# A four-layer graph network: the first layer's sums with all 14 cells' rows of a pair of batches gathered by TensorE, without indirect DMAs

## What is computed

```
def spmm(edge_row, edge_col, edge_val, m):
    gathered = edge_val[:, None] * m[edge_col]
    return jax.ops.segment_sum(gathered, edge_row, num_segments=N_NODES)
h = jax.nn.relu(spmm(edge_row, edge_col, edge_val, x @ W1))
out = spmm(edge_row, edge_col, edge_val, h @ W2)
x = _layernorm(x + out)
...
x = _layernorm(x + _L0_gnn_ref(x, src, dst, edge_weight, W1, W2))
x = _layernorm(x + _L1_gnn_ref(...))   # typed edges
x = _layernorm(x + _L2_gnn_ref(...))   # weighted edges, tanh map
x = _layernorm(x + _L3_gnn_ref(...))   # attention
```

## Time and profile before

| | us |
|---|---|
| timed runs, median of 3 | 9364.93 |
| timed runs, lowest and highest | 9363.02, 9368.05 |
| profiled execution, span | 12999.9 |
| profiled execution, anything beside its span | not shown |
| busy in the profiled span: TensorE, VectorE, ScalarE, GpSimd | 9231.9, 6869.4, 3183.5, 5674.7 |

### The profile page before, as it was taken

One profiled execution on the slowest core, in us unless ns is written; L12 is line 12 of the kernel. 1 busy time (PEld: TensorE's weight loads), 2 busy tenths in 40 slices (PEclk: granted clock), 3 DMA queues, 4 the chain that ended last, 5 costly groups with the idle time before them and its releaser, 6 DMA issues. The chain is left out here.

```text
span 12999.9 us, 294862 instructions
## 1 busy us (share of the span) xinstructions
PE 9231.9 (71%) x88712; PEld 7531.3 (58%) x88762; DVE 6869.4 (53%) x25269; ACT 3183.5 (24%) x9441; POOL 5674.7 (44%) x5790
## 2 busy tenths in 40 slices
PE   5977777777777777677777774888873555555555
PEld 5866667776766667634454453666662444444443
DVE  8964444444444444456666665555544555555555
ACT  5841111112111111241111123111113233222223
POOL 3534444442444444305555551444442555555552
PEclk8888888888888888789999996888886555555555
DMA  1013333333333333462222223333332111111113
GB/s 50 28 47 90 91 89 89 88 90 105 90 89 90 89 88 90 95 217 69 67 67 66 67 70 110 101 104 102 101 94 70 39 39 39 39 39 39 39 39 61
DMA packets 962709, 999.47 MB, mean 77 GB/s; under 512 B 141701, under 2 KB 861933, under 8 KB 962093
## 3 DMA queue, kind: packets, MB, share of 16 engines
q1 hardware_dynamic: 774502, 616.47, 17.1%
q0 software_dynamic: 174720, 364.70, 12.9%
q10 hardware_dynamic: 13255, 16.19, 0.4%
HBM read 858.52 MB, written 144.69 MB: 77 GB/s over the span
## 5 line engine op out<-in xcount | busy, mean ns | idle before, releaser
L497 POOL DMA_INDIRECT ring<-att_table,idx x1592 | 1556.3, 978 | 1307.7 <-ACT idx L484 715.5
L1225 PE MATMUL psum<-ring 128*128 128x128 bf16 x21276 | 1547.8, 226 | 784.6 <-issue 766.3
L1225 PEld LDWEIGHTS psum<-ring 128*128 128x128 bf16 x21276 | 1281.3, 101 | 984.9 <-issue 927.9
L1162 DVE TENSOR_SCALAR ring<-sel,iota_col 128x640 bf16<-128x640 bf16 (+1 forms) x1576 | 487.0, 369 | 2368.2 <-remote 1627.6
L1240 PE MATMUL psum<-state 64*128 64x128 f32 x14112 | 1479.8, 356 | 208.9 <-issue 206.7
L1240 PEld LDWEIGHTS psum<-state 64*128 64x128 f32 x14112 | 1318.1, 261 | 345.7 <-issue 330.0
L1148 POOL DMA_INDIRECT ring<-gcn_table,idx x980 | 932.3, 951 | 1300.6 <-ACT idx L1197 996.0
L1679 POOL DMA_INDIRECT state<-rel_table,state x1120 | 1071.1, 956 | 981.8 <-ACT state L1779 657.6
L1148 POOL DMA_INDIRECT ring<-rows,idx x980 | 933.7, 953 | 1289.0 <-ACT idx L1197 993.2
L1169 DVE TENSOR_SCALAR state<-iota_row,state 128x128 f32<-128x128 f32 x5488 | 1457.2, 356 | 0.0
L1394 POOL DMA_INDIRECT state<-hyp_table,state x784 | 755.8, 964 | 855.3 <-ACT state L1471 650.6
(11 more groups left out here) (447 smaller groups left out, 15814.7 us busy)
## 6 DMA issues: line engine op xcount, KB each, us to landing
ring<-xparts SPq DMA_DIRECT2D x1332, 192.0 KB
ring<-srow SPq DMA_DIRECT2D x544, 128.0 KB
sel<-drow SPq DMA_DIRECT2D x394, 160.0 KB
sel<-drow SPq DMA_DIRECT2D x394, 128.0 KB
rel_table<-tout SPq DMA_DIRECT2D x98, 512.0 KB, 2.6
ring<-att_table,idx POOLq DMA_INDIRECT x1592
ring<-rows SPq DMA_DIRECT2D x56, 448.0 KB
xparts<-state SPq DMA_DIRECT2D x28, 672.0 KB, 3.6
```

Source lines behind the costliest of these rows:

```text
L497: pool.indirect_dma_start(out=ring[:, u, k, 0:width], out_offset=None, in_=table, in_offset=bass.IndirectOffsetOnAxis(ap=idx[:, u, k:k + 1 ...
L1162: ins = nc.vector.tensor_scalar(reach[u % 2][:, t, :], wanted[u], at[:, :], None, ALU.is_equal)
L1225: last = nc.tensor.matmul(rowsP[v][:, j * P:(j + 1) * P], reach[v][:, t, j * P:(j + 1) * P], xwin[u][:, t, i, :], start=(t + i == 0), stop ...
```

## The change

For every cell the gather now takes place on TensorE. `PC`, `JP` and `JQ` are gone; `wanted`, `reach`, `rowsP` and `got` have all 7 x 128 = 896 columns (`BC`) for both batches of a pair; GpSimd's block, ScalarE's `stage`, the buffers `fetched` and `fetch` and their filling go; `scatter` takes all rows from `got` and waits for no indirect DMA. The rest of `cell_pass` is the same. The diff, without a few lines of its context:

```diff
--- before.py
+++ after.py
@@ -45,16 +45,11 @@
 GC = 28
 GW = GC // 2
 HS = P // 2
-JQ = (2, 3)
-JP = (SJ - JQ[0], SJ - JQ[1])
-QA = (0, JQ[0])
-QP = JQ[0] + JQ[1]
 GB = -(-(-(-E // P)) // GC)
 assert GB % 4 == 0 and (GB + 1) * GC <= EC and AW * SW <= NPAD and AW <= P
 CELLS = SG * GB * SJ
 CT = -(-(CELLS + 2 * SJ) // P)
 BC = SJ * P
-PC = (JP[0] * P, JP[1] * P)
 TOP = TILES * P - SW
 OFF = 1.0e6
 FG = 7
@@ -634,8 +629,6 @@
         assert at + 8 <= RING * K * ROW5
         tout_flat = tout[:, :, :].rearrange("p a w -> p (a w)")
         iota256 = tout_flat[:, 2 * RELS * D - SW:2 * RELS * D]
-        FETCH = (SG * GB // 2 + 1) * QP
-        fetch = state[:, NPAD - FETCH:NPAD]
         spread = tout_flat[0:GC, 0:GC * P // 2].bitcast(BF16).rearrange("p (c e) -> p c e", e=P)
 
         PT = 2
@@ -982,17 +975,6 @@
                             to.rearrange("p (g j i) -> p g j i", j=SJ, i=FB),
                             cells(tabW)[:, :, FR + q * FB:FR + (q + 1) * FB, :].rearrange("p g i j -> p g j i"))
                     ins.then_inc(sem("made"), 1)
-                    dve.wait_ge(sem("tbuilt"), -(-(CT + FT) // 4))
-                    indirect = cells(node[:, 0:CELLS])[:, :, :, min(JP):SJ]
-                    c(nc.vector.tensor_tensor(
-                        indirect, indirect,
-                        gbase.unsqueeze(1).unsqueeze(3).to_broadcast([P, SG, GB, SJ - min(JP)]), ALU.add))
-                    pairs = node[:, 0:CELLS].rearrange("p (q v j) -> p q v j", v=2, j=SJ)
-                    lists = fetch[:, 0:SG * GB // 2 * QP].rearrange("p (q i) -> p q i", i=QP)
-                    for v in range(2):
-                        c(nc.vector.tensor_scalar(lists[:, :, QA[v]:QA[v] + JQ[v]], pairs[:, :, v, JP[v]:SJ],
-                                                  float(N - 1), None, ALU.min))
-                    c(nc.vector.memset(fetch[:, SG * GB // 2 * QP:FETCH], 0.0))
 
                 @block.tensor
                 def _(pe):
@@ -1086,9 +1068,8 @@
 
         after[0] = 2 * CELLS
         picks = [in_state(SJ * P).rearrange("p (j d) -> p j d", d=P) for _ in range(4)]
-        got = [in_state(PC[u % 2]) for u in range(4)]
-        assert after[0] <= NPAD - FETCH
-        wanted = [sel_flat[:, u * (BC // 2):u * (BC // 2) + PC[u % 2] // 2].bitcast(BF16) for u in range(4)]
+        got = [in_state(BC) for u in range(4)]
+        wanted = [sel_flat[:, u * (BC // 2):(u + 1) * (BC // 2)].bitcast(BF16) for u in range(4)]
 
         def in_ring(words):
             at, ring_at[0] = ring_at[0], ring_at[0] + words
@@ -1097,9 +1078,8 @@
 
         ring_at = [0]
         xwin = [in_ring(3 * D).bitcast(BF16).rearrange("p (t i f) -> p t i f", t=2, i=3) for _ in range(4)]
-        reach = [in_ring(PC[v]).bitcast(BF16).rearrange("p (t e) -> p t e", t=2) for v in range(2)]
+        reach = [in_ring(BC).bitcast(BF16).rearrange("p (t e) -> p t e", t=2) for v in range(2)]
         zeros_b = in_ring(256).bitcast(BF16)
-        fetched = [in_ring(JQ[u % 2] * D).rearrange("p (q f) -> p q f", f=D) for u in range(4)]
         SUMS = SJ * SW
 
         def cell_pass(table):
@@ -1109,7 +1089,7 @@
 
 
             sums = [psum[:, 2 * h:2 * h + 2, :].rearrange("p b c -> p (b c)")[:, 0:BC] for h in range(2)]
-            rowsP = [psum[:, 4 + 2 * v:6 + 2 * v, :].rearrange("p b c -> p (b c)")[:, 0:PC[v]]
+            rowsP = [psum[:, 4 + 2 * v:6 + 2 * v, :].rearrange("p b c -> p (b c)")[:, 0:BC]
                      for v in range(2)]
             LAST = SG * GB
             IT = GB // 4
@@ -1124,7 +1104,7 @@
                                      xparts[bass.ds(at, SW), :].rearrange("(t p) c -> p t c", p=P)
                                      ).then_inc(sem(f"xin{u}"), 16)
                         sp.wait_ge(sem("reach"), n + 1)
-                        sp.dma_start(wanted[u], drow[bass.ds(n * BC, PC[u % 2])].partition_broadcast(P)
+                        sp.dma_start(wanted[u], drow[bass.ds(n * BC, BC)].partition_broadcast(P)
                                      ).then_inc(sem(f"din{u}"), 16)
 
                     with sp.Fori(0, SG) as sg:
@@ -1136,22 +1116,6 @@
                             load(LAST + u, GB + u, u)
                         sp.wait_ge(sem(f"xin{u}"), (LAST // 4 + (u < 2)) * 16)
                         sp.wait_ge(sem(f"din{u}"), (LAST // 4 + (u < 2)) * 16)
-
-                @block.gpsimd
-                def _(pool):
-                    with pool.Fori(0, SG) as sg:
-                        with pool.Fori(0, IT) as it:
-                            for u in range(4):
-                                pool.wait_ge(sem("staged"), sg * GB + it * 4 + (u + 1))
-                                pool.sem_inc(sem("issued"), 1)
-                                for q in range(JQ[u % 2]):
-                                    pool.indirect_dma_start(
-                                        out=fetched[u][:, q, :], out_offset=None, in_=table,
-                                        in_offset=bass.IndirectOffsetOnAxis(ap=idx[:, u, q:q + 1], axis=0)
-                                    ).then_inc(sem(f"g{u}"), 16)
-                    for u in range(4):
-                        pool.wait_ge(sem(f"g{u}"), LAST // 4 * 16 * JQ[u % 2])
-                    pool.dma_reset(range(sem("g0").num, sem("g3").num + 1))
 
                 @block.vector
                 def _(dve):
@@ -1192,13 +1156,6 @@
 
                 @block.scalar
                 def _(act):
-                    def stage(n, u, at):
-                        act.wait_ge(sem("scat"), n + 1)
-                        nc.scalar.activation(idx[:, u, 0:JQ[u % 2]], fetch[:, bass.ds(at, JQ[u % 2])],
-                                             ACT.Copy).then_inc(sem("staged"), 1)
-
-                    for u in range(2):
-                        stage(u, u, QA[u])
                     with act.Fori(0, SG) as sg:
                         with act.Fori(0, IT) as it:
                             for u in range(0, 4, 2):
@@ -1208,9 +1165,6 @@
                                     act.wait_ge(sem("scat"), n + (v + 1))
                                     nc.scalar.activation(got[u + v], rowsP[v], ACT.Copy
                                                          ).then_inc(sem("got"), 1)
-                                for v in range(2):
-                                    stage(n + (v + 2), (u + v + 2) % 4,
-                                          sg * (GB // 2 * QP) + it * (2 * QP) + ((u // 2 + 1) * QP + QA[v]))
 
                 @block.tensor
                 def _(pe):
@@ -1219,7 +1173,7 @@
                         pe.wait_ge(sem("reach"), n + 5)
                         pe.wait_ge(sem(f"xin{u}"), loaded)
                         pe.wait_ge(sem("got"), n + 1)
-                        for j in range(JP[v]):
+                        for j in range(SJ):
                             for t in range(2):
                                 for i in range(3):
                                     last = nc.tensor.matmul(rowsP[v][:, j * P:(j + 1) * P],
@@ -1228,14 +1182,11 @@
                                                             start=(t + i == 0), stop=(t + i == 3))
                         last.then_inc(sem("gat"), 1)
 
-                    def scatter(n, u, fetches):
+                    def scatter(n, u):
                         pe.wait_ge(sem("got"), n + 3)
                         pe.wait_ge(sem("picked"), n + 1)
-                        own = JP[u % 2]
                         for j in range(SJ):
-                            if j == own:
-                                pe.wait_ge(sem(f"g{u}"), fetches)
-                            rows = got[u][:, j * P:(j + 1) * P] if j < own else fetched[u][:, j - own, :]
+                            rows = got[u][:, j * P:(j + 1) * P]
                             for h in range(2):
                                 last = nc.tensor.matmul(sums[h][:, j * P:(j + 1) * P],
                                                         rows[h * HS:(h + 1) * HS, :],
@@ -1262,8 +1213,7 @@
                                 pe.wait_ge(sem("sent"), sg + 1)
                                 clear(True)
                             for v in range(2):
-                                q = 16 * JQ[v]
-                                scatter(n + v, u + v, sg * (IT * q) + it * q + (at // 4 * q + q))
+                                scatter(n + v, u + v)
 
                     pe.sem_inc(sem("gat"), 4)
                     pe.sem_inc(sem("scat"), 4)
```

## The result

The changed kernel takes 10060.94 us (median of 4 runs, 10058.7 to 10064.46), against 9366.49 us for the kernel before (4 runs, 9363.02 to 9375.23): 694 us more, a ratio of 1.074 with a 95% interval of 1.0726 to 1.0755. The forecast was 10040, its range 9700 to 10150.

A forecast was written before the change was run, and what follows sets the result against it. TensorE was taken to bound the changed stage at 6.51 us a pair. Gathers +680, run-ahead gathers at the calls' starts +3.5 and setup -2.5 gave +681 on 9365, 10046, stated as 10040 us; range 9700 to 10150.

The forecast's parts named there:

- The bound: Changed stage, timed run: TensorE sets the pair's period at 6.51 us, GpSimd just behind at 6.25 us.
- that cover: Per pair of the changed stage: TensorE outlasts GpSimd's indirect DMAs by 0.26 us, so removing them gains nothing.
- rival A: GpSimd already bounds the timed pair, at 6.9 to 7.5 us; changed kernel 9655 to 9890 us; chance 0.13.
- T: True period of one pair in the changed stage before the change: taken as 6.51 us, at most 9.28.
- the 11.37 us of the table by stage: Recorded time a pair in the stretched profile: 4456 us over 392 pairs of the changed stage's two calls.
- rival B: TensorE's gaps during the gather are real, made by indirect DMAs; break-even or faster, 8957 at the limit; chance 0.10.
- (1): Gather on TensorE: 30 more matmuls a pair at 57.8 ns, 1.73 us unhidden, +680 us over 392 pairs.
- (6): GpSimd and ScalarE: 1960 indirect DMAs, 2450 us of GpSimd's time, and index copies go; costed at nothing.
- (3, 4): VectorE comparisons grow to 456 ns each, ScalarE copies to 927 ns, both hidden under the scatter.
- (5): Row loads: hardware queue grows from 2.65 to 3.3 us a pair, the software queue's 1.8 us goes.
- (7): Setup: four VectorE operations, 1.37 us, and three smaller go, about -2.5 us.

The follow-up runs named there:

- the first experiment: Kernel before, unedited, profiled a second time: the execution took 9365.33 us with a span of 9363.5 us.
- the changed kernel with spare fetches: Changed kernel plus five indirect DMAs a pair into a spare buffer nobody reads or waits for: 10056.54 us, ratio 1.074 to the kernel before.

## Why the prediction was right, point by point

- **The bound.** TensorE at 6.51 us, GpSimd at 6.25 behind it. Measured 6.446, the same without any indirect DMA; a sixth puts GpSimd in front. GpSimd's 6.25 was its quickest pace: under load its DMAs start 1.27 to 1.29 us apart, so it stood 0.1 us behind at most and not 0.26. The forecast did not hang on the size of that cover, but it was much nearer to rival A than the prediction thought. Taking T from the one pair without gaps was the step that carried everything; the 11.37 us of the table by stage would have led to rival B. That the other stages run in 0.80 of their recorded time was nearly right too: they were put at 6813 us and measure about 6755 (9363.5 less 1297.0 + 1298.5 and, behind each call's last gather, one pair). The two calls are some 56 us longer than the 2552 us put on them, by their starts and the 12 seams, which the prediction did not count; both kernels have these.
- **The gathers (1).** 30 x 57.8 ns = 1.73 us a pair. Measured 8.120 - 6.446 = 1.674 us, 55.8 ns a matmul, and the steps of six matmuls between four, five and six indirect DMAs give 55.7 and 55.8: a straight line with 3.43 us of the pair left for everything else. The prediction's 57.8 ns had taken a fixed part of the gather's 3.12 us into the price of a matmul. The difference is 22 us in the sum of 680. The Trainium skill's 81 ns ("TensorE: Matmul & The Clock Gate", "Back-to-back issue gap") would have given 953 us, and these rows disagree with it for this stream.
- **The removal (6), at nothing.** Shown from both sides: taken from the kernel before, 1.0004; put back into the changed one, no difference.
- **Comparisons and copies (3, 4).** 450 ns against 456, 918 against 927, and under the scatter as said. That TensorE would wait for comparisons at the starts and seams, the prediction did not see: 54.6 us in the changed kernel. The kernel before, in the trace without gaps, has 54.5, so the change adds nothing to it.
- **Queues (5).** 3.0 us a pair for 3.3 forecast.
- **The sum came out closer than its parts.** Between the traces of the first experiment and of the changed kernel lie 10056.5 - 9363.5 = 693.0 us. The two calls between their first and last gathers account for 661.0 us (1627.1 and 1629.4 against 1297.0 and 1298.5); what lies before the first of them for 3.0, where 2.5 less were forecast (7); what lies between the calls for 0.5; and 28.5 lie behind the second call's last gather, in stages that the change does not touch. One row shows the largest part, the indirect DMAs of the typed layer, in the kernel before and in the changed one (line, count, min/median/max ns, first and last start):

```profile
L1679 POOL DMA_INDIRECT state<-rel_table,state x1120: 938/944/1762, 3958.0 to 5485.8; - x187
```

```profile
L1629 POOL DMA_INDIRECT state<-rel_table,state x1120: 939/946/1077, 4623.8 to 6170.7; - x187
```

1527.8 us from first to last there and 1546.9 here, with the same median of one. In the nine traces taken the same stage has 1517.6 to 1558.3 us, the longest in the changed kernel with spare fetches. The prediction had counted nothing here. So its 680 + 3.5 us for the calls was 23 us too large and a term of 28 us was missing: the mechanism was right, and that the sum of 681 stands within 12 us of the measured 693 is in part luck.

**Left open.** Why the unchanged typed stage takes up to 40 us more in some of these kernels was not tried, so it is not known whether the change has a part in those 28.5 us. Nor is it known what stretched the first profiled execution of the kernel before: nine more, of this kernel and of the others, each have a span within 3 us of the time of their own execution. Recording as such thus does not bring the gaps. That it was a full record pipeline (the Trainium skill's "NOTIFIC — the notification-queue block", on overflow) is not shown and not excluded.

## What to carry to other kernels

If a profile's span and the timed runs disagree, look for the stretch whose work runs without gaps and take the period from there; the mean over the stage, 11.37 us a pair, pointed here to rival B, to no change or a gain. Work on an engine that does not set the period was worth nothing when it went, even where that engine had no pause either, and the work that replaced it on the bound was paid in full: find that out by taking the one away without adding the other. And look at seams between loops: an addition in program order ahead of the next trip's first inputs stood in front of TensorE twelve times and brought its clock down behind some of the waits. Moving it gave 52 us in the two calls, 0.6%.

## What was not expected of the hardware

- 145 GB/s instead of 105, with indirect DMAs among them, moved beside TensorE at the same 8.12 us a pair.
- GpSimd's indirect DMAs started 1.25 us apart at their quickest and 1.27 us in the mean when six a pair made it the bound.
- A wait of the same 3.1 us was followed by the low clock at seven of twelve seams and not at the other five, 1.6 us each time.
- A pair's period was constant to a nanosecond or two over hundreds of pairs (6.446 to 6.447 us from the 1st to the 90th percentile), which made 6 matmuls of 56 ns measurable in a trace of 9.4 ms.
- Stages that no edit touches varied by up to 38 us between kernels. A difference under 0.4% between two kernels of this size should be placed in the trace before it is believed.
